# Graph passes of a GNN kernel: one TensorE event per gathered group, one or two per count stretch, where there were up to ten

## The chip, the cores and the metric

The kernel runs on one core of one Trainium2 chip. The metric is device time of the whole program in microseconds (us), the median of repeated runs. One more execution was recorded by the hardware profiler; the rows below are from it.

## The reference, cut to what matters

The program is a chain of four blocks on 6250 nodes with 256 features. The change touches only the first, a hypergraph convolution applied twice over 106250 edges (`src` to `dst`, sorted by `dst`; both directions of 50000 random pairs, and a loop at each node):

```python
def _hypergraph_conv(x, hei, W, b, num_nodes, num_edges):
    src, he = hei[0], hei[1]
    xw = x @ W.T
    deg_n = segment_sum(ones, src); deg_e = segment_sum(ones, he)
    edge_feat = b_inv[:, None] * segment_sum(xw[src], he)
    out = d_inv[:, None] * segment_sum(edge_feat[he], src)
    return out + b
...
out = _prelu(_hypergraph_conv(x, W1, b1), a)
out = _prelu(_hypergraph_conv(out, W2, b2) + x, a)
```

Each convolution is two sums over neighbours, so there are four passes over the graph, s1 to s4. A recurrent network, an attention over the same edges and a mixture of experts follow.

## The kernel before, in words

`stage_row_pass` is one pass. It makes 49 blocks of 128 summed rows in two ways, as **items**:

- A **D item** ("count stretch", 24 of them, the first 24 blocks of 128 nodes) multiplies a dense matrix of edge counts with the whole table of rows: 49 matmuls of 128x512, in 7 chunks of 7 matmuls. A chunk of counts is loaded as bf16 by SyncE (SP) into `staged` (7 slots, `CR`), widened to fp32 by ScalarE (ACT, `widen`, L621) into `ring` (3 slots, `WR`), and used by TensorE (PE, L1072).
- A **G item** ("gathered group", 54 of them) fetches 8 tiles of 128 rows by 8 indirect DMAs that GpSimd (POOL) issues (L519) into `rows` (3 buffers), and sums them by 8 one-hot matmuls (L1056). Before them one matmul "opens" the sum with the last tile of the group before (`open_sum`, L1043).

After each item, ACT copies the sum out of PSUM (L662), VectorE (DVE) scales it, and in s1, s2 and s4 PE turns the row block (L1003); in s1 and s2 it also multiplies it by a weight (`make`, L1020), ACT copies both results (L568, L575), and stores the block by a DMA (L592). These steps of earlier items stand in the middle of a later item on PE.

The order is written out by hand (`order_of_items`). In s2, s3 and s4 three G items lead, and then 2 or 3 G items stand ahead of each D item. In s1 the counts are only being built: 24 G items lead, POOL then scatters the counts by 416 indirect DMAs (L528) in four quarters, and D items 0 to 16 run as one chain, released by quarters 1 (D 0 to 4), 2 (D 5 to 10) and 3 (D 11 to 16). Then 7 D items and 30 G items are mixed, D 17 first. POOL scatters before it gathers group 24. In s1, DVE also adds the 7 chunks of a D item (`sum_chunks`, L874, L878) for the degrees.

PE tells others of its progress by semaphore increments, here called **events**. Before the change it sends, in each pass: `freed` and `group_done` for a G item (108), `a_used` for each of the 7 chunks of a D item (168), `turned` (78 in s1, s2 and s4), `made` (78 in s1 and s2), and `column_out` (24 in s1).  `freed` is what POOL waits for before it gathers into a buffer again; `a_used` is what `widen`, the loads of SP, and the copy of a D item wait for.

## Time and profile before

| | us |
|---|---|
| median of 3 runs | 6864.92 |
| lowest and highest | 6851.33, 6879.35 |
| span of the profiled execution, first to last instruction | 6729.2 |
| median less that span | 135.7 |
| PE busy, POOL busy in the span | 4418.9 (66%), 3355.7 (50%) |
| mean granted TensorE clock, share of full speed | 0.812 |

The profile gives the span alone; what lies around it is taken as the 135.7 us by which the median is above it. The four passes stand from about 60 to 3990 us. The rest of the program, to 6729 us, is not touched.

### The profile page before, as it was taken

The numbers are of one execution on the slowest core, as the hardware profiler recorded it, in microseconds if no ns is written. First come the engines' busy times: TensorE is split into PE (matmuls) and PEld (weight loads), VectorE is DVE, ScalarE is ACT, GpSimd is POOL, SyncE is SP. The second block draws the span as 40 slices with busy tenths as digits, with TensorE's granted clock in tenths as the row PEclk, the third lists the DMA queues.
The fourth block names the chain that finished last, engine by engine and source line by source line (L and its number), as shares of the span: only waits on it lengthen the run. The fifth ranks groups of instructions, "written<-read, shape, count | busy, mean of one in ns | idle before, by whom it ended". The sixth has DMA issues, their size and how long they took to land. (4 is left out here: it accounts for less than half of the span.)

```text
span 6729.2 us, 72351 instructions
## 1 busy us (share of the span) xinstructions
PE 4418.9 (66%) x20150; PEld 3518.5 (52%) x20150; DVE 2669.2 (40%) x6797; ACT 1559.4 (23%) x3386; POOL 3355.7 (50%) x3423
## 2 busy tenths in 40 slices
PE   3611139766778867876766659998546666666399
PEld 2410027554666646665555549996424444444287
DVE  7610026322222221112444342225566666666544
ACT  1100025212232222322222224333300000001233
POOL 5677730555455555655544421112466666662555
PEclk8755569878888888987888879998767777777599
DMA  7800024435444445555555550710554444444255
GB/s 265 255 18 11 11 62 120 123 107 167 128 134 131 133 148 158 162 149 167 166 166 161 154 159 0 201 38 4 147 139 117 119 118 121 118 120 118 100 88 88
DMA packets 523908, 822.38 MB, mean 122 GB/s; under 512 B 92040, under 2 KB 428367, under 8 KB 520055
## 3 DMA queue, kind: packets, MB, share of 16 engines
q0 software_dynamic: 158784, 367.62, 21.0%
q1 hardware_dynamic: 269235, 331.42, 16.5%
q10 hardware_dynamic: 95588, 120.03, 5.5%
q8 instruction: 102, 1.67, 0.1%
q14 instruction: 199, 1.63, 0.1%
HBM read 658.73 MB, written 198.82 MB: 127 GB/s over the span
## 5 line engine op out<-in xcount | busy, mean ns | idle before, releaser
L1072 PE MATMUL s_part<-both_halves,s_ring 128*128 128x512 f32 x4704 | 1330.9, 441 | 934.8 <-issue 467.3
L519 POOL DMA_INDIRECT acc<-table,ids x1296 | 1265.4, 976 | 1050.5 <-PE s_part L1043 634.7
L1072 PEld LDWEIGHTS s_part<-both_halves,s_ring 128*128 128x128 f32 x4704 | 984.3, 214 | 1217.9 <-issue 559.7
L1953 POOL DMA_INDIRECT at_rows<-h_t,ids x832 | 807.8, 971 | 470.4 <-issue 249.1
L1056 PE MATMUL s_part<-acc 128*128 128x257 f32 x3456 | 907.8, 411 | 148.5 <-DMA acc<-table,ids 59.0
L1056 PEld LDWEIGHTS s_part<-acc 128*128 128x128 f32 x3456 | 707.7, 210 | 278.2 <-DMA acc<-table,ids 64.8
L621 ACT ACTIVATE s_ring<-acc 128x896 fp32r<-128x896 bf16 x672 | 612.1, 945 | 886.3 <-remote 329.6
L519 POOL DMA_INDIRECT acc<-xn_d,ids x432 | 431.6, 999 | 495.3 <-PE s_part L1043 338.6
L2358 PE MATMUL at_part<-at_rows,at_onehot 128*128 128x264 f32 x1664 | 604.6, 493 | 4.1 <-DVE at_onehot L2175 4.1
L725 DVE TENSOR_TENSOR acc<-acc 128x256 f32<-128x256 f32 x96 | 40.9, 426 | 1376.9 <-ACT acc L662 1376.3
L528 POOL DMA_INDIRECT counted<-acc,s_place x416 | 427.2, 1027 | 132.0 <-issue 128.6
L662 ACT ACTIVATE acc<-s_part 128x257 f32<-128x257 f32 (+1 forms) x312 | 140.3, 450 | 1177.4 <-issue 316.8
L2358 PEld LDWEIGHTS at_part<-at_rows,at_onehot 128*128 128x128 f32 x1664 | 371.5, 244 | 75.1 <-issue 11.8
L1551 POOL COPY acc<-h 128x125 f32 x160 | 66.7, 417 | 598.3 <-DVE h L1579 598.3
L793 DVE TENSOR_TENSOR acc<-s_fixed,rel 128x1024 f32<-128x1024 f32 x216 | 263.9, 1222 | 195.0 <-ACT acc L662 148.5
L874 DVE TENSOR_TENSOR acc<-acc 128x896 f32<-128x896 bf16 (+1 forms) x144 | 158.2, 1098 | 430.3 <-DMA acc<-counted 361.7
L2168 DVE TENSOR_TENSOR at_rows<-at_rows,at_ps_w 128x1024 f32<-128x1024 f32 x208 | 250.7, 1205 | 34.0 <-issue 33.5
L2784 POOL DMA_INDIRECT out<-ex_y,ex_ids x112 | 178.6, 1595 | 165.1 <-DMA out<-ex_y,ex_ids 102.3
L1020 PE MATMUL s_psY<-acc 128*128 128x256 f32 x624 | 182.5, 419 | 118.2 <-issue 43.2
L1020 PEld LDWEIGHTS s_psY<-acc 128*128 128x128 f32 x624 | 123.6, 206 | 146.9 <-issue 63.7
L1995 ACT ACTIVATE at_raw<-at_part 128x264 f32<-128x264 f32 x104 | 40.6, 390 | 670.4 <-remote 246.5
L1496 PE MATMUL sw_ps<-xs,wih 128*128 x1600 | 188.3, 276 | 1.2 <-PEq L1452 1.2
(418 smaller groups left out, 6172.7 us busy)
## 6 DMA issues: line engine op xcount, KB each, us to landing
acc<-counted SPq DMA_DIRECT2D x672, 224.0 KB
xs_d<-blank SPq DMA_DIRECT2D x38, 1032.0 KB
counted<-in_x ACTq DMA_DIRECT2D x24, 1568.0 KB
table<-acc ACTq DMA_DIRECT2D x214, 128.0 KB
acc<-table,ids POOLq DMA_INDIRECT x1299
both_halves<-table SPq DMA_DIRECT2D x21, 896.0 KB, 11.9
ex_x<-xs_d SPq DMA_DIRECT2D x60, 258.0 KB
at_rows<-h_t,ids POOLq DMA_INDIRECT x832
```

The source lines that it names most:

```text
L519: pool.indirect_dma_start(rows[:, j % R, k, 0:D], None, table[0:NP_, :], bass.IndirectOffsetOnAxis(cst["ids"][:, t:t + 1], 0)).then_inc(ro ...
L528: pool.indirect_dma_start(cst["counted_flat"], bass.IndirectOffsetOnAxis(place[:, q, k:k + 1], 0), times_out[:, q, k:k + 1], None, bounds_ ...
L621: act.activation(chunk(n).bitcast(F32R), staged[:, n % CR, :], ACT.Copy).then_inc(widened, 1)
L793: dve.tensor_tensor(onehot[:, j % OG], iota.unsqueeze(1).to_broadcast([P, JT, P]), cst["rel"][:, 1, JT * g:JT * g + JT].unsqueeze(2).to_br ...
L1020: ins = pe.matmul(psY[:, 0:D], turned_x[k % 2][:, h, :], w[:, h, :], start=(h == 0), stop=(h == 1))
L1056: ins = pe.matmul(part[i % 4][:, 0:D + 1], onehot[:, k % OG, t, :], rows[:, k % R, t, 0:D + 1], start=False, stop=(t == JT - 1))
L1072: ins = pe.matmul(part[i % 4][:], chunk(n)[:, b * P:(b + 1) * P].bitcast(F32R), both[:, c * BG + b].bitcast(F32R), start=(c == 0 and b == ...
L1496: pe.matmul(ps[u][half][:, q * C:(q + 1) * C], wih[:, kk, col:col + P], xs[:, kk, bass.ds(step, 1), :].rearrange("p a c -> p (a c)"), star ...
L1953: pool.indirect_dma_start(rows[:, t % AHEAD, :], None, table, bass.IndirectOffsetOnAxis(cst["ids"][:, t:t + 1], 0)).then_inc(rows_in[t % A ...
L2168: dve.tensor_tensor(rv[:, :, 0:D].rearrange("p t (h d) -> p t h d", h=H8), rv[:, :, 0:D].rearrange("p t (h d) -> p t h d", h=H8), ps_w[:, ...
L2358: ins = pe.matmul(part[k][:, 0:W], onehot[:, t, :], row, start=(t % JT == 0), stop=False)
L2784: pool.indirect_dma_start(out, bass.IndirectOffsetOnAxis(ids[u][:, c:c + 1], 0), y[u][:, c, :], None, compute_op=ALU.add).then_inc(added[u ...
```

## The change

- PE's events: one at the end of each G item (on the next group's opening matmul, where that follows), one at the end of each D item, and for D items "in parts" one more behind their second chunk. `freed`, `a_used`, `group_done`, `turned`, `made` and `column_out` are gone; all who waited for them wait for `item_done`. Items behind the last have one event each.
- The ring has 5 slots. In s1 the first 16 D items (`LONG`) are "whole": they have 7 slots, and send one event. The two more slots lie in the gather buffers, so that group 24 isn't gathered before D item 15 is done.
- ACT widens 5 chunks of the next D item (7 where whole) at the end of the current D item, and the last two behind the event in its middle. `staged` has 5 slots (was 7), freed by `widened`, which ACT itself sends.
- A row block is turned 3 items behind its sum (was 2 in s1, s2), and multiplied and stored 5 behind (was 3).
- In s1 the degrees are turned by DVE (a copy and a 32x32 transpose), not by a PE matmul and an ACT copy; DVE finishes item i two items later; their store has 4 pieces.

```diff
-CR = 7
-WR = 3
+CR = 5
+WR = 5
+LONG = 16
...
-        LAG = 3 if kind == "last" else 2
+    R, OG, LA, LAG = 3, 3, 2, 3
+    MK = LAG + 2
...
+        def whole(win):
+            return builds and win < LONG
...
+        done = [0]
+        for i in range(NI + trailing):
+            done.append(done[i] + (2 if i < NI and in_parts(i) else 1))
+        def wait_for_part(eng, i):
+            eng.wait_ge(item_done, done[i + 1] - 1)
+        def wait_for_item(eng, i):
+            eng.wait_ge(item_done, done[i + 1])
...
                 if n >= CR:
-                    sp.wait_ge(a_used, n - CR + 1)
+                    sp.wait_ge(widened, n - CR + 1)
...
             def gather(j):
-                if j >= R - 1:
-                    pool.wait_ge(freed, j - R + 2)
+                if j >= R:
+                    wait_for_item(pool, at_g[j - R] if opens_next(j - R) else at_g[j - R + 1])
+                if builds and j == FIRST_G:
+                    wait_for_item(pool, at_d[LONG - 1])
...
             def copy_turned(k):
-                act.wait_ge(turned, k + 1)
-                if makes and k >= 2:
-                    act.wait_ge(made, k - 1)
...
             def copy_made(k):
-                act.wait_ge(made, k + 1)
...
             def widen(n):
                 act.wait_ge(a_in[n % CR], 16 * (n // CR + 1))
-                if n >= WR:
-                    act.wait_ge(a_used, n - WR + 1)
...
+                if is_d and in_parts(i):
+                    wait_for_part(act, i)
+                    for n in range(NG * win + WR, NG * win + NG):
+                        widen(n)
+                if i < NI + trailing:
+                    wait_for_item(act, i)
...
+                store_due(i)
+                if is_d and win + 1 < DW:
+                    for n in range(NG if whole(win + 1) else WR):
+                        widen(NG * win + NG + n)
...
+                        if counts:
+                            link(dve.tensor_copy(deg_col[:, 0:1], times_in))
+                            if i >= ND:
+                                wait_for_row_of(dve, i - ND)
+                            link(dve.transpose(deg_row[i % ND], deg_col))
...
-                        ins.then_inc(group_done, 1)
-                        if k + 1 < GS and at_g[k + 1] - i <= 3:
-                            open_sum(k + 1, at_g[k + 1])
+                        if opens_next(k):
+                            ins = open_sum(k + 1, at_g[k + 1])
+                        ins.then_inc(item_done, 1)
...
-                            ins.then_inc(a_used, 1)
+                            if c == NG - WR - 1 and in_parts(i):
+                                ins.then_inc(item_done, 1)
+                        ins.then_inc(item_done, 1)
```

On ACT, in the chain of D items of s1, the rows from one copy of a D sum to what follows it were these (`s_part` is the sum, `s_psT` and `s_psY` a block turned and multiplied, `s_ring` the widened counts; each row with the semaphores it waits for):

```order
L662 ACTIVATE acc<-s_part 128x512 [waits s1_scaled,s1_a_used]
L621 ACTIVATE s_ring<-acc 128x896 [waits s1_a_used,s1_a_in0]
L621 ACTIVATE s_ring<-acc 128x896 [waits s1_a_used,s1_a_in1]
L621 ACTIVATE s_ring<-acc 128x896 [waits s1_a_used,s1_a_in2]
L621 ACTIVATE s_ring<-acc 128x896 [waits s1_a_used,s1_a_in3]
L621 ACTIVATE s_ring<-acc 128x896 [waits s1_a_used,s1_a_in4]
L564 ACTIVATE acc<-s_psT 1x128 [waits s1_g_stored,s1_made,s1_turned]
L568 ACTIVATE acc<-s_psT 128x256
L575 ACTIVATE acc<-s_psY 128x257 [waits s1_g_stored,s1_made]
L621 ACTIVATE s_ring<-acc 128x896 [waits s1_a_used,s1_a_in5]
L621 ACTIVATE s_ring<-acc 128x896 [waits s1_a_used,s1_a_in6]
```

At the same place of the changed kernel (L675 is the copy, L591 and L596 the other two copies, L613 and L616 the stores, L640 the widening):

```order
L675 ACTIVATE acc<-s_part 128x512 [waits s1_scaled,s1_item_done]
L591 ACTIVATE acc<-s_psT 128x256
L596 ACTIVATE acc<-s_psT 128x256 [waits s1_g_stored]
L613 ISA [waits s1_g_stored,s1_made_out]
L613 DMA table<-acc 128x256
L616 REGISTER_ALU [waits s1_ready]
L616 DMA deg_d<-acc 4x32
L640 ACTIVATE s_ring<-acc 128x896 [waits s1_a_in4]
L640 ACTIVATE s_ring<-acc 128x896 [waits s1_a_in0]
L640 ACTIVATE s_ring<-acc 128x896 [waits s1_a_in1]
L640 ACTIVATE s_ring<-acc 128x896 [waits s1_a_in2]
L640 ACTIVATE acc_counts<-acc 128x896 [waits s1_a_in3]
```

One wait for PE is left for a D item, where each widening had one; all widening stands behind the stores now.

On ACT in s2, around one D item, the rows before were:

```order
L662 ACTIVATE acc<-s_part 128x257
L621 ACTIVATE s_ring<-acc 128x896 x2
L568 ACTIVATE acc<-s_psT 128x256
L575 ACTIVATE acc<-s_psY 128x256
L621 ACTIVATE s_ring<-acc 128x896 x2
L592 DMA table<-acc 128x256
L662 ACTIVATE acc<-s_part 128x512
L621 ACTIVATE s_ring<-acc 128x896 x3
```

and in the changed kernel, from the copy of the G item ahead:

```order
L675 ACTIVATE acc<-s_part 128x257
L591 ACTIVATE acc<-s_psT 128x256
L596 ACTIVATE acc<-s_psT 128x256
L613 DMA table<-acc 128x256
L640 ACTIVATE acc_counts<-acc 128x896
L640 ACTIVATE s_ring<-acc 128x896
L675 ACTIVATE acc<-s_part 128x512
```

Two chunks, not four, are widened while the D item runs.

## Rows read from the trace of the kernel before

**Rows 1.** Busy us of PE, PEld, DVE, ACT, POOL in s1 to s4; clock, DMA.
```profile
60.00:1560.00 1500.00, 732.73 (x2820) 543.48 (x2820) 475.01 (x765) 256.79 (x487) 856.40 (x846) 0.73 0.34 100
1560.00:2402.00 842.00, 643.86 (x2621) 520.16 (x2621) 214.57 (x494) 244.79 (x410) 422.24 (x433) 0.87 0.47 138
2402.00:3122.00 720.00, 550.70 (x2148) 438.97 (x2148) 134.84 (x329) 195.71 (x253) 421.29 (x434) 0.88 0.53 156
3122.00:3990.00 868.00, 583.98 (x2298) 464.36 (x2299) 375.40 (x1017) 227.60 (x403) 424.68 (x432) 0.82 0.56 164
```
**Rows 2.** Waits of POOL for PE in s2, s3, s4: total us, times, longest.
```profile
POOL acc L519 <- PE s_part L1043: 238.5, 22, 15.8
...
POOL acc L519 <- PE s_part L1043: 121.3, 18, 15.6
...
POOL acc L519 <- PE s_part L1043: 274.8, 22, 17.2
```
**Rows 3.** Timeline of POOL: scatter begins, gathering of group 24 begins, two restarts.
```profile
343.42 1.03 POOL L528 DMA_INDIRECT counted<-acc,s_place  x1 [3.33 <-DVEq L849]
...
899.53 0.99 POOL L519 DMA_INDIRECT acc<-xn_d,ids  x1 [0.30 <-issue]
...
1168.92 0.95 POOL L519 DMA_INDIRECT acc<-xn_d,ids  x1 [248.53 <-PE s_part L1043]
...
1523.04 0.94 POOL L519 DMA_INDIRECT acc<-xn_d,ids  x1 [13.86 <-PE s_part L1043]
```
**Rows 4.** Timeline of ACT in the scatter: start, duration, idle time before and releaser.
```profile
538.30 0.27 ACT L564 ACTIVATE acc<-s_psT 1x128 f32<-1x128 f32 x1 [40.29 <-issue]
...
616.70 0.60 ACT L662 ACTIVATE acc<-s_part 128x512 f32<-128x512 f32 x1 [57.79 <-issue]
...
781.96 0.60 ACT L662 ACTIVATE acc<-s_part 128x512 f32<-128x512 f32 x1 [57.85 <-remote]
```
**Rows 5.** Timeline of SP's load issues in the scatter, and busy time there.
```profile
557.90 0.32 SPq L498 DMA_DIRECT2D acc<-counted  x1
...
597.10 0.32 SPq L498 DMA_DIRECT2D acc<-counted  x1
...
343.00:895.00 552.00, 72.27 (x201) 49.71 (x199) 34.97 (x47) 24.74 (x41) 423.85 (x413) 0.55 0.06 12
```
**Rows 6.** Timeline of s1 with POOL silent (923 to 1160).
```profile
1051.46 5.01 PE L1072 MATMUL s_part<-both_halves,s_ring 128*128 128x512 f32 x21 [1.62 <-ACT s_ring L621]
...
1064.66 0.60 ACT L662 ACTIVATE acc<-s_part 128x512 f32<-128x512 f32 x1 [3.75 <-PE s_part L1072]
...
1079.46 0.60 ACT L662 ACTIVATE acc<-s_part 128x512 f32<-128x512 f32 x1 [3.76 <-PE s_part L1072]
```
**Rows 7.** Timeline of one D item of s3 while POOL issues three groups.
```profile
2661.29 5.14 PE L1072 MATMUL s_part<-both_halves,s_ring 128*128 128x512 f32 x21
...
2669.73 0.95 ACT L621 ACTIVATE s_ring<-acc 128x896 fp32r<-128x896 bf16 x1 [6.70 <-DMA acc<-in_x]
2680.25 0.95 ACT L621 ACTIVATE s_ring<-acc 128x896 fp32r<-128x896 bf16 x1 [9.56 <-DMA acc<-in_x]
```
**Rows 8.** Two openings of G items in s2, back to back.
```profile
1856.04 0.60 PE L1043 MATMUL s_part<-acc 128*128 128x257 f32 x2
...
1861.03 0.60 PE L1043 MATMUL s_part<-acc 128*128 128x257 f32 x2
```
**Rows 9.** L1072 in 1640:2380 (s2), 2500:3100 (s3), 3190:3940 (s4).
```profile
L1072 PE MATMUL s_part<-both_halves,s_ring x1114: 387/393/796, 1639.4 to 2368.4; 128*128 128x512 f32 x186
...
L1072 PE MATMUL s_part<-both_halves,s_ring x1078: 387/389/797, 2508.5 to 3090.5; 128*128 128x512 f32 x180
...
L1072 PE MATMUL s_part<-both_halves,s_ring x1079: 387/392/988, 3196.6 to 3939.7; 128*128 128x512 f32 x180
```
**Rows 10.** Timeline of POOL: one gather instruction in s3, and the idle time before it.
```profile
2740.61 0.95 POOL L519 DMA_INDIRECT acc<-table,ids  x1 [0.30 <-issue]
```
**Rows 11.** Waits of PE in s4, 3190:3940, before turning a block.
```profile
PE s_psT L1003 <- issue: 63.0, 12, 11.7
```

More of the change, by code:

```diff
@@ L343, in stage_row_pass @@
     counts = degrees is not None and kind == "edge"
+    trailing, late = MK if makes else LAG if turns else 0, 2 if builds else 0
     per_store = 32 if counts else 16
@@ L378, in stage_row_pass @@
             psY = m.ps(f"{name}_psY", [P, 512])
-            y = [room.take(D + 1) for _ in range(NY)]
-        if counts:
-            deg_row = [room.take(P)[0:1, :] for _ in range(2)]
+            y = [room.take(D) for _ in range(NY)]
         if kind != "edge":
@@ L997, in turn @@
                     pe.wait_ge(turned_out, k - 1)
[L998 to L1001 removed]
+                frm = x[k % NX] if makes else row[b]
                 for h in range(2):
                     ins = pe.transpose(psT[b][:, h * P:(h + 1) * P], frm[:, h * P:(h + 1) * P], cst["ident"][:])
[L1004 removed]
@@ L1006, in column_of, with make @@
-            def column_of(k, narrow):
-                if not narrow:
-                    pe.matmul(psY[:, D:D + 1], cst["ident"][:], cst["ones"][:, 0:1], start=True, stop=True)
-                    return
+                return ins
+            def make(k):
+                pe.wait_ge(turned_out, k + 1)
+                if k >= 2:
+                    pe.wait_ge(made_out, k - 1)
+                for h in range(2):
+                    ins = pe.matmul(psT[k % 2][:, D:2 * D], turned_x[k % 2][:, h, :], w[:, h, :], start=(h == 0),
+                                    stop=(h == 1))
+                return ins
@@ L1010, in column_of, with make_and_turn @@
+            def make_and_turn(i):
+                if makes and MK <= i < NI + MK:
+                    ins = make(i - MK)
+                if turns and LAG <= i < NI + LAG:
+                    ins = turn(i - LAG)
+                if i >= NI:
+                    ins.then_inc(item_done, 1)
+            def column_of(i):
+                k = items[i][1]
                 pe.wait_ge(column_ready, k + 1)
-                pe.matmul(psY[:, D:D + 1], total_sum, cst["ones"][:, 0:1], start=True, stop=True).then_inc(column_out, 1)
@@ L1013, in make @@
-            def make(k, narrow):
-                pe.wait_ge(turned_out, k + 1)
                 if k:
-                    pe.wait_ge(made_out, k)
-                if with_column(k):
-                    column_of(items[k + 2][1], narrow)
-                for h in range(2):
-                    ins = pe.matmul(psY[:, 0:D], turned_x[k % 2][:, h, :], w[:, h, :], start=(h == 0), stop=(h == 1))
-                ins.then_inc(made, 1)
-            def make_and_turn(i, narrow=True):
-                if makes and i >= 3:
-                    make(i - 3, narrow)
-                if turns and LAG <= i < NI + LAG:
-                    turn(i - LAG, narrow)
+                    pe.wait_ge(scaled, at_d[k - 1] + 1)
```

229 lines of the change are left out of this document (110 added, 119 removed).

## Prediction

> **What bounds the kernel now.** I first read the busy time by pass [rows 1]. The passes take 1500, 842, 720 and 868 us, and nothing in them is busy throughout: in s2, PE works 644 of 842 us and POOL 422. (POOL's 0.30 us between two DMAs belongs to its pace: one gather instruction takes 0.95 + 0.30 = 1.25 us [rows 10], a group of 8 takes 10.0, and 54 groups 540.) The reader is to see that s2, s3 and s4 stand 180 to 330 us above POOL's 540.
>
> The table of waits came second [rows 2]: POOL waits for PE 238 us in s2, 121 in s3, 275 in s4. So PE is late, though it is idle for a quarter of the time. Why it is late shows in the timeline [rows 7]. A D item starts at 2661.29 and does 3 chunks in 5.1 us. The fourth and fifth chunk need a ring slot, freed by `a_used` of the first and second, which PE had finished by about 2664.7. ACT, idle, goes on at 2669.73 and at 2680.25: 7 to 16 us after the matmuls that it waits for. The counts had long been loaded. What is late is PE's event.
>
> The scatter of s1 shows the same with a rhythm [rows 4, 5]. SP issues its loads every 19.6 us (557.90 to 597.10 in two steps), each when one more `a_used` reaches it, and ACT copies a D sum at 616.70 and at 781.96, 165.3 us apart. PE is busy 72 of 552 us there [rows 5]. A D item sends 10 events in this stretch (7 `a_used`, `turned`, `made`, `column_out`), and 165.3 us is 8.4 times 19.6. With POOL silent, the copy at 1064.66 follows the last matmul by less than 0.1 us, and a D item takes 14.8 us [rows 6]. So I read it thus: while POOL issues DMAs, PE's events go out one by one, at 19.6 us in the scatter and some 5 to 10 us in a long run of gathers [rows 7], and PE's own number of events sets the pace.
>
> **A rule that speaks against this.** The Trainium skill (TensorE: Matmul & The Clock Gate, "The cost: per-tile semaphore tail") says that increments by matmuls serialize at 26.3 ns each. The change takes away about 1118 events, and by that rule this would be worth 29 us, an estimate from that page. By the trace one event costs up to 19.6 us [rows 5]. The trace and the page differ by far more than a hundred times while POOL is busy. With POOL silent the trace [rows 6] does not contradict the page.
>
> **Count of events.** Before: 54 x 2 + 24 x 7 = 276 in s3; with `turned` 354 in s4, with `made` too 432 in s2, with `column_out` 456 in s1: 1518. After: 54 + 2 x 24 = 102 in s3 and s4, 107 in s2, and in s1 54 + 16 + 2 x 8 + 5 = 91: about 400.
>
> **Prices of PE's work at full clock.** 21 count matmuls take 5.01 us [rows 6], so 49 take 11.7. A G item of s2 takes 1861.03 - 1856.04 = 4.99 us [rows 8], with one make and turn. PE's busy time differs between s2 and s3 by (643.9 - 550.7)/78 = 1.2 us an item and between s4 and s3 by 0.4 [rows 1]. So s2: G 5.0, D 12.9; s3: G 3.8, D 11.7; s4: G 4.2, D 12.1.
>
> **s1, until group 24 is gathered.** The scatter stands from 343 to 899.5 [rows 3] and is unchanged. D 0 starts at 478. A whole D item sends one event. After it ACT copies the sum (0.60), two blocks, issues two stores and widens the first chunk (0.95): about 3.5 us before PE can go on, since whole items share all 7 slots; before, the next item's first chunks stood ready but for the ring. With PE's 12.9 and a little this is 17 us an item with POOL silent, against 14.8 now: a loss. In the scatter I add 2.5 us for matmuls at a lower clock, and for the event half of 19.6: 29.3 us, against 165. D 0 to 4 end at 625, D 5 to 10 (released well before) at 801, and by 899.5 14.4 of the 16 items are done, where now fewer than 3 are. The rest takes 1.6 x 17 = 27: group 24 is gathered from 927. Bounds: event at once, 899.5 (all 16 are done at about 881); event after the full 19.6, 39 us an item, 10.8 done, 5.2 x 17 more: 988.
>
> **s1, the 30 groups behind.** Now POOL restarts at 1168.92 with 28 to go and restarts last at 1523.04 [rows 3]: (1533 - 1169)/28 = 13.0 us a group. Every two groups it waits. With fewer events I expect three groups between waits of 3 us, that is (3 x 10.3 + 3)/3 = 11.3, taken as 11.2; a group is 10.3 us here, 8 x (0.99 + 0.30) [rows 3]. 927 + 30 x 11.2 = 1263 against 1533: **-270**. Bounds: 899.5 + 30 x 10.3 = 1209 (-324), and 988 + 30 x 13 = 1378 (-155).
>
> **s2, s3, s4.** One D item comes with 2.25 G items. The time of such a stretch now is the window over (count of matmuls / 49) [rows 9]: s2 740/22.7 = 32.6 us, s3 600/22.0 = 27.3, s4 750/22.0 = 34.1. After:
> - s2: PE 2.25 x 5.0 + 12.9 = 24.1. The event in the middle of D is sent 3.4 us in, comes after up to 8 us [rows 7], and ACT widens in 1: 12.4, while five chunks cover 8.4 + 1.2. So 3 us of stall remain: 27.1. Over 24 stretches **-132**. Bounds: no stall, 24.4 (-195); stall 6 (-60).
> - s3: PE 2.25 x 3.8 + 11.7 + 3 = 23.3, but POOL needs 22.6, plus a wait of 2.5 us for every two groups: 25.4, **-46**. Bounds: POOL without waits 23.1 (-100); no gain.
> - s4: 2.25 x 4.2 + 12.1 = 21.6, plus 3 and the 63 + some us that PE waits before turning [rows 11], 4.4 a stretch with what stands beside it. That rests on DVE's chain of ten steps, not on events alone, so I keep it and half a microsecond more for ACT: 29.5, **-110**. Bounds: POOL's 25.4 (-208), and -60.
>
> **Small terms.** Two more widenings before the first item of three passes, 2 x 0.95 x 3 = 6; two more trailing items in s1 and s2, some 1.5 us each: **+12** in all. The degrees on DVE cost two short instructions an item, hidden: DVE is busy 475 of 1500 us [rows 1]. Staging 5 slots, not 7, costs nothing while loads land 2 us after their issue and are freed by ACT's own events; if cover were gone, two loads (4 us) for each D item, 24 x 4 a pass.
>
> **Sum.** -270 - 132 - 46 - 110 + 12 = -546. The profiled span of 6729.2 becomes 6183, and with the 135.7 us around it the median 6319.
>
> **Rivals.**
> - *POOL alone bounds.* Events no longer queue at all: all four upper bounds, -827 + 12, so about 6050; with half of that extra gain 6185. For it: short stretches of the trace where events come within 1 us. Against it: a POOL that never waits is just where events were slowest.
> - *The scatter does not speed up.* If it is the loads that take 19.6 us there (224 KB each; only 12 GB/s are moved), D items keep their pace and s1 gains only 28 x 1.8 = 50. Total -326, 6539. Against it: once issued, loads land in about 2 us, and ACT's copy, which needs no load, keeps the same rhythm [rows 4].
> - *Events cost only themselves* (the page's rule). Nothing but tens of ns for each of 1118: 6835, no measurable change. The trace speaks against it [rows 4, 7].
> - *Slower: POOL's longer runs starve the one event that a D item needs.* Today a D item gets through because POOL stops every two groups. If the event in its middle comes only when POOL stops, after three groups, a stretch takes 3 x 10 + 3, and the next D the same: some 36 us in s2 and s4, 36 in s3: 24 x (3.4 + 8.7 + 1.9) = +336; less s1's 270 that is +66, 6930. It decides from 546/80 = 6.8 us of extra stall for each of the 80 D items in parts, so from about 9.8 us each.
>
> **Chances.** The forecast (6200 to 6450) 0.58; POOL alone bounds 0.18; scatter unchanged 0.15; events cost only themselves 0.05; slower 0.04. The range 6100 to 6580 leaves out the last two and the far end of the second. A measurement of this kernel can't tell less than about 0.5% (34 us) from no change: faster 0.91, same 0.05, slower 0.04.
>
> **What the profile after would show.** Right: copies of D sums (L675, 512 wide) every 25 to 40 us in the scatter, not 165; group 24 gathered by 900 to 990, s1 ended by about 1300; POOL's waits in s2 and s4 halved; PE's stalls before the sixth chunk some 3 us. Wrong: D items still 100 us or more apart in the scatter; POOL in runs of three groups with PE idle more than 8 us within each D item; or PE waiting on `psT` and `made_out` in s2 as it waits now for the ring.

## The result and the profile after

The changed kernel takes 6753.68 us (median of 4, 6734.97 to 6758.35), where the kernel before took 6867.65 us in the same comparison: a ratio of 0.9837, interval 0.9812 to 0.9861. It is 114 us (1.7%) faster, where 546 us were forecast.

The same kernel takes a different time on different chips: the kernel before was met at about 6868, at 6720 to 6745, and at 5495 to 5500 us. So every ratio below is to the kernel before on the same chip. "The 5500 us chips" names the last kind (B in some expectations, where A is the 6868 us kind); it needs a reading of its own.

The page of the changed kernel, its first line:

```profile
span 6733.3 us, 71038 instructions
```

The time of that execution is 6734.97 us, so only 1.7 us lie around a span. The 135.7 us that the prediction took for "around the span" were not that: the profiled execution of before was itself some 134 us shorter than those timed.

Windows by pass of the changed kernel, answering [rows 1], with the same columns (busy us of PE, PEld, DVE, ACT, POOL, then clock, DMA share, GB/s):

```profile
60.00:1604.00 1544.00, 725.67 (x2664) 557.24 (x2664) 498.91 (x899) 235.31 (x409) 839.13 (x846) 0.71 0.33 97
1604.00:2410.00 806.00, 655.24 (x2621) 514.87 (x2621) 213.02 (x494) 235.73 (x410) 419.99 (x433) 0.88 0.47 144
2410.00:3136.00 726.00, 572.49 (x2148) 446.92 (x2148) 134.79 (x329) 189.43 (x253) 420.20 (x433) 0.85 0.50 155
3136.00:3960.00 824.00, 576.60 (x2258) 459.25 (x2259) 374.33 (x1012) 217.57 (x400) 427.10 (x433) 0.83 0.57 173
```

Against [rows 1], pass s1 is longer by about 44 us, s2 and s4 are shorter by about 36 and 44, and s3 is 6 longer. That does not add up to 114 us, and the two spans are nearly the same (6729.2 and 6733.3): the profile of before is of a shorter execution than its timed runs, so this comparison can't place the gain. Waits of POOL for PE, in s2, s3 and s4 of the changed kernel, answering [rows 2]:

```profile
POOL acc L549 <- PE s_part L1065: 205.4, 22, 12.9
...
POOL acc L549 <- PE s_part L1065: 128.0, 18, 15.6
...
POOL acc L549 <- PE s_part L1065: 235.1, 23, 14.4
```

They are as many as before (22, 18 and 22 then), and their sum is 14% smaller in s2 and s4. The halving that was forecast for s2 and s4 is not to be seen. Nor are three groups between waits in s1: in the 28 groups from 1206 us on, POOL waits 14 more times.

ACT's copies of D sums in the scatter of the changed kernel, answering [rows 4]:

```profile
608.40 0.60 ACT L675 ACTIVATE acc<-s_part 128x512 f32<-128x512 f32 x1 [121.91 <-remote]
768.34 0.60 ACT L675 ACTIVATE acc<-s_part 128x512 f32<-128x512 f32 x1 [151.47 <-remote]
924.13 0.60 ACT L675 ACTIVATE acc<-s_part 128x512 f32<-128x512 f32 x1 [147.35 <-remote]
```

and the busy time there, answering [rows 5]:

```profile
343.00:895.00 552.00, 67.96 (x191) 45.15 (x191) 30.86 (x44) 22.59 (x33) 400.52 (x408) 0.53 0.06 12
```

This is the finding of the profile after. A D item in the scatter now sends one event, and not ten, and the copies still stand 159.9 us apart, where they stood 165.3 apart (the third came at 924.13, when the scatter had ended). The timeline of PE between the first two copies shows why:

```profile
611.97 7.10 PE L1100 MATMUL s_part<-both_halves,s_ring 128*128 128x512 f32 x21 [91.22 <-issue]
618.91 1.02 PE L1031 MATMUL s_psT<-acc 128*128 128x256 f32 x4
619.77 0.38 PE L1023 MATMUL s_psT<-ident,s_x 128*128 128x128 f32 x2
619.91 1.85 PE L1100 MATMUL s_part<-both_halves,s_ring 128*128 128x512 f32 x7
...
632.53 0.59 PE L1100 MATMUL s_part<-both_halves,acc_counts 128*128 128x512 f32 x1 [2.21 <-issue]
635.33 0.58 PE L1100 MATMUL s_part<-both_halves,acc_counts 128*128 128x512 f32 x1 [2.21 <-issue]
...
680.13 0.58 PE L1100 MATMUL s_part<-both_halves,acc_counts 128*128 128x512 f32 x1 [2.22 <-issue]
```

PE has all operands: all 7 chunks of a whole item are widened before its last matmuls. It takes some 35 instructions at its own speed, and then one every 2.80 us, with nothing that it waits for by the profile ("issue"). The last one starts at 680.13, and its event reaches ACT at 768.34: 87.6 us after the end, or 31 times 2.80 (one item earlier the same: from 520.16 to 608.40). I read this so: ends are told every 2.80 us, and PE starts instructions some 31 ahead of those whose end is told. The count of instructions here is that of the trace: a count matmul is one, while a matmul by a one-hot matrix, by the weight or for the degrees stands as two (L1056 has 3456, which is 2 x 8 for each of 216 groups). So a D item has 49 matmuls and, from L1031, L1023 and the sum for the degrees (L1049), 4 + 2 + 2 more: 57 x 2.80 = 159.6, measured 159.9. Before it had 59: 165.2, measured 165.3.

POOL in the changed kernel, answering [rows 3]: the scatter's last instruction, the start of groups 24 and 25, the restart with group 26, and the first gather of s2:

```profile
904.51 0.98 POOL L558 DMA_INDIRECT counted<-acc,s_place  x1 [0.41 <-issue]
1159.25 0.99 POOL L549 DMA_INDIRECT acc<-xn_d,ids  x1 [253.77 <-PE s_part L1100]
...
1206.13 0.95 POOL L549 DMA_INDIRECT acc<-xn_d,ids  x1 [27.03 <-PE s_part L1065]
...
1604.30 0.95 POOL L562 DMA_INDIRECT acc<-table,ids  x1 [29.91 <-POOLq L356]
```

Two of the sixteen whole D items are done at the end of the scatter, a third soon after it, and group 26 starts 37 us later than it did (1168.92 in [rows 3]).

With POOL silent, each of the other thirteen takes 18.0 us on average (copies from 924.13 to 1158.47), where an item took 15.0 (943.68 to 1138.65). PE at the start of one of them, and the windows 960:1150 of before and of the changed kernel:

```profile
1018.78 6.66 PE L1100 MATMUL s_part<-both_halves,s_ring 128*128 128x512 f32 x21 [3.28 <-ACT s_ring L640]
...
960.00:1150.00 190.00, 168.98 (x758) 131.74 (x757) 121.45 (x155) 98.99 (x143) 0.00 (x0) 1.00 0.43 117
...
960.00:1150.00 190.00, 153.30 (x595) 122.08 (x594) 106.83 (x143) 78.81 (x110) 0.00 (x0) 0.87 0.33 100
```

PE is idle for 3.28 us there, where it was for 1.62 [rows 6], because the first widening of the next item stands behind ACT's two copies and two stores. The next 21 matmuls then take 6.66 us and not 5.01, and the granted clock of that stretch is 0.87, where it was 1.00.

### The profile page after: what moved, and what is told of

It reads as the page before. It is cut to its first block and busy times, and to the rows that moved or that the text cites. A ratio compares the mean times of both kernels' runs of the same rounds, so it can differ in the third digit from the quotient of the medians.

```text
span 6733.3 us, 71038 instructions
## 1 busy us (share of the span) xinstructions
PE 4446.3 (66%) x19994; PEld 3536.5 (53%) x19994; DVE 2693.7 (40%) x6935; ACT 1515.0 (23%) x3308; POOL 3342.7 (50%) x3423
## 5 line engine op out<-in xcount | busy, mean ns | idle before, releaser
L1100 PE MATMUL s_part<-both_halves,s_ring 128*128 128x512 f32 x3598 | 1029.0, 435 | 748.5 <-issue 494.1
L1100 PEld LDWEIGHTS s_part<-both_halves,s_ring 128*128 128x128 f32 x3598 | 743.9, 210 | 978.7 <-issue 705.1
L1082 PE MATMUL s_part<-acc 128*128 128x257 f32 x3456 | 988.7, 432 | 322.7 <-issue 162.2
L1082 PEld LDWEIGHTS s_part<-acc 128*128 128x128 f32 x3456 | 734.7, 219 | 501.5 <-issue 216.5
L675 ACT ACTIVATE acc<-s_part 128x257 f32<-128x257 f32 (+1 forms) x312 | 138.5, 447 | 2095.0 <-remote 1004.4
L640 ACT ACTIVATE s_ring<-acc 128x896 fp32r<-128x896 bf16 x514 | 455.2, 938 | 545.4 <-remote 180.7
L558 POOL DMA_INDIRECT counted<-acc,s_place x416 | 409.8, 985 | 155.0 <-issue 155.0
L1100 PE MATMUL s_part<-both_halves,acc_counts 128*128 128x512 f32 x1106 | 326.8, 429 | 171.0 <-issue 138.0
L1100 PEld LDWEIGHTS s_part<-both_halves,acc_counts 128*128 128x128 f32 x1106 | 223.3, 205 | 235.2 <-issue 157.5
L1065 PE MATMUL s_part<-acc 128*128 128x257 f32 x432 | 142.3, 411 | 70.2 <-issue 23.7
```

Source lines behind the costliest of these rows:

```text
L558: pool.indirect_dma_start(cst["counted_flat"], bass.IndirectOffsetOnAxis(place[:, q, k:k + 1], 0), times_out[:, q, k:k + 1], None, bounds_ ...
L640: act.activation(chunk(n).bitcast(F32R), staged[:, n % CR, :], ACT.Copy).then_inc(widened, 1)
L1082: ins = pe.matmul(part[i % 4][:, 0:D + 1], onehot[:, k % OG, t, :], rows[:, k % R, t, 0:D + 1], start=False, stop=(t == JT - 1))
L1100: ins = pe.matmul(part[i % 4][:], chunk(n)[:, b * P:(b + 1) * P].bitcast(F32R), both[:, c * BG + b].bitcast(F32R), start=(c == 0 and b == ...
```

## The experiments

### One question: what is paced, events or instructions?

**More events.** The kernel before, with one more increment on each of 6 of a chunk's 7 matmuls, 42 for a D item, 4032 in all:

```diff
+        extra = m.sem(f"{name}_extra")
...
+                                if b < BG - 1:
+                                    ins.then_inc(extra, 1)
```

The expectations call the prediction's reading E (events are paced) and the new one M (ends of instructions are paced). The first is that of the unchanged kernel, run to learn where the 134 us between its profile and its timed runs lie. It met a 5500 us chip, so it could not answer that; more_events met such chips three times.

> The kernel before, unchanged, to see where its time stands in an execution near its median. The profile of before that the prediction used spans 6729 us, 138 us below the median of 6868, and the changed kernel's spans 6733. Both theories (E: while GpSimd issues DMAs, TensorE's events go out one by one and their number sets the pace; M: what is slow is the completion of each TensorE instruction, 2.8 us in the scatter, whatever it signals) expect about 6850 to 6880 us here, with the 110 to 140 us more somewhere between 60 and 3990 us; if the span is again near 6730, the gain of the change is not in the passes at all.

> The kernel before, with 42 more semaphore increments in each D item (on every count matmul that had none, on a semaphore for which nobody waits). E: in the scatter a D item sends 52 events, not 10, and takes 52 x 19.6 = 1020 us or at least several times 165; the program is slower by hundreds of us or more. M: the number of instructions is the same, D items stay 165 us apart in the scatter, and the time stays within 1% of before.

> The kernel before with 42 more increments in each D item (4032 in all). On B they cost 2 us in all at most, as before (5497 against 5495). On A: E expects D items in the scatter several times the 165 us apart, and hundreds of us more; M expects 165 us and a time within 1% of before.

> The kernel before with 42 more increments in each D item. On B again within 8 us of before. On A: E expects D items in the scatter several times the 165 us apart, and hundreds of us more; M expects 165 us and a time within 1% of before.

Measured: unchanged 5495.64; with more events 5497.22, 5502.83 and 5508.66 us, where the kernel before took 5495.29, 5496.63 and 5500.24. That is 2 to 8 us for 4032 events, at most 2.1 ns each, from single runs and hardly outside the spread of the kernel before (5489 to 5505), and on these chips nothing of PE is late in the scatter in the first place: D copies stand 14.8 us apart there too. So this could not tell the theories apart. A chip of the other sort was met later.

> The kernel before with 42 more increments of a semaphore per wide item, 4032 in all. If this chip is one where the kernel before takes about 6870 us: by events being paced, the copies of wide items in the scatter stand several hundred us apart; by each instruction's end being paced, they stand 165 us apart as before and the time is within 20 us of the kernel before. If it is one where the kernel before takes about 5500 us: no difference of over 10 us by either.

Measured: 6755.67 us, the kernel before 6743.41; ratio 1.0019 (0.9990 to 1.0048). Timeline of PE in the scatter, from one D item's first matmul to the last one before the next copy (L1073 counts, L1012 and L1001 the sums of degrees and their turn, L1021 multiply, L1004 turn):

```profile
616.60 6.35 PE L1073 MATMUL s_part<-both_halves,s_ring 128*128 128x512 f32 x21 [55.96 <-ACT s_ring L622]
635.68 0.59 PE L1012 MATMUL s_psY<-ones,acc 128*128 128x1 f32 x2 [12.73 <-ACT s_ring L622]
636.13 2.06 PE L1021 MATMUL s_psY<-acc 128*128 128x256 f32 x4
638.12 0.58 PE L1001 MATMUL s_psT<-ident,acc 128*1 128x128 f32 x2
638.63 0.69 PE L1004 MATMUL s_psT<-ident,acc 128*128 128x128 f32 x2
638.97 2.28 PE L1073 MATMUL s_part<-both_halves,s_ring 128*128 128x512 f32 x7
655.28 3.35 PE L1073 MATMUL s_part<-both_halves,s_ring 128*128 128x512 f32 x7 [14.03 <-issue]
703.51 3.35 PE L1073 MATMUL s_part<-both_halves,s_ring 128*128 128x512 f32 x7 [44.87 <-issue]
722.48 3.36 PE L1073 MATMUL s_part<-both_halves,s_ring 128*128 128x512 f32 x7 [15.62 <-ACT s_ring L622]
```

and of ACT, the two copies around it:

```profile
615.02 0.60 ACT L663 ACTIVATE acc<-s_part 128x512 f32<-128x512 f32 x1 [57.79 <-issue]
780.28 0.60 ACT L663 ACTIVATE acc<-s_part 128x512 f32<-128x512 f32 x1 [57.85 <-remote]
```

52 events instead of 10, and the copies are 165.26 us apart as before, to the hundredth. Events are not what is paced. The rows of PE sum to 59 instructions, and 59 x 2.80 = 165.2. The 19.6 us on which I built fit the same: a chunk has 7 matmuls, 7 x 2.80 = 19.6.

**Fewer instructions.** The changed kernel with 4 of the 7 matmuls of each chunk. It leaves out 3 of 7 blocks of nodes.

```diff
-                            for b in range(BG):
+                            for b in range(BG - 3):
```

> The changed kernel with 4 of the 7 matmuls of each count chunk (28 a D item, 21 left out of 49, so the counts of 3 blocks of nodes in 7 are left out of the sums). Events and loads are as in the changed kernel. M: in the scatter a D item is 28 + 8 = 36 TensorE instructions of 2.8 us, so 101 us from copy to copy, not 160. E or loads: 155 to 160 us stays. In s2 to s4 both expect less time, 21 x 0.24 = 5 us a D item by TensorE's work alone (-360 us over 72 items), M more than that where GpSimd is issuing.

> The changed kernel with 4 of the 7 matmuls of each count chunk (21 of 49 left out, so 3 blocks of nodes in 7 are left out of the sums). On A: M expects 36 instructions x 2.8 = 101 us from copy to copy in the scatter, E 155 to 160. On B: 5481 again.

On 5500 us chips it took 5481.49 and 5490.27 us, 14 and 6 below the kernel before and 85 and 76 below the changed kernel (5566.25 on one such chip, below), where the expectation had 360 less in s2 to s4: PE's own work is not all that bounds the passes there. On a 6868 us chip:

> The changed kernel with 4 of the 7 matmuls of each chunk (it leaves out 3 of 7 blocks of nodes), so a wide item has 36 of TensorE's instructions and not 57. If the end of each instruction is paced at 2.80 us in the scatter: copies of wide items 101 us apart there. If something per item or per event is paced: 160 us apart as before. On a chip without the pacing: as in the runs before, within 15 us of the kernel before.

Measured: 6393.05 us, ratio 0.9312 (0.9276 to 0.9348). Timeline of ACT in its scatter:

```profile
654.74 0.60 ACT L675 ACTIVATE acc<-s_part 128x512 f32<-128x512 f32 x1 [92.67 <-remote]
755.84 0.60 ACT L675 ACTIVATE acc<-s_part 128x512 f32<-128x512 f32 x1 [92.67 <-remote]
```

101.1 us apart (the next is 101.2 later), and 36 x 2.80 = 100.8. Nothing per item, per chunk, per load or per event fits 165.3, 159.9 and 101.1; 2.80 us for each instruction fits all three.

It reaches further than the scatter. Beside the changed kernel on the same chip (6763.02 us) the run is 370 us shorter: s1 ends 116 us sooner, and s2, s3 and s4 are 110, 78 and 63 us shorter. On the 5500 us chips the same edit makes them 34, 8 and 25 us shorter (four_of_seven2 beside after_again). So the number of PE's instructions also costs more in the gather passes where ends are told late.

**A quarter of the scatter.** The changed kernel with 104 scattering DMAs for 416. It leaves out three quarters of the counts.

```diff
-                        sp.wait_ge(scattered[q], 16 * QT)
+                        sp.wait_ge(scattered[q], 16 * (QT // 4))
...
-                for k in range(QT):
+                for k in range(QT // 4):
```

> The changed kernel with a quarter of the scatter's instructions, 104 for 416 (it leaves out three quarters of the counts). Theory (TensorE's instructions end late while GpSimd scatters, and by that alone): the scatter takes about 140 us and not 565; at most one wide item's copy comes late, the others stand 17.6 us apart from then on, and the run is 350 to 450 us faster than the changed kernel. Rival (something else of that stretch paces them, the loads of counts or the stretch of the program): the copies stand 160 us apart behind the scatter's end too, and the gain is under 200 us.

Measured: 6364.21 us, beside 6763.02 for the changed kernel on the same chip: 399 us less. POOL's last scattering DMA, and the first two D copies:

```profile
470.25 0.98 POOL L558 DMA_INDIRECT counted<-acc,s_place  x1 [0.30 <-issue]
...
505.27 0.60 ACT L675 ACTIVATE acc<-s_part 128x512 f32<-128x512 f32 x1 [9.79 <-PE s_part L1100]
523.19 0.60 ACT L675 ACTIVATE acc<-s_part 128x512 f32<-128x512 f32 x1 [9.45 <-PE s_part L1100]
```

17.9 us apart as soon as the scatter is over, and 17.4 to 19.1 for the ones that follow (once 23.7). The pacing goes with the scatter. It shows that POOL's scatter, with what it sets off, slows the ends of PE's instructions on such a chip; it does not show by which path. POOL's own pace is not what differs between chips: it issues the 416 DMAs of the scatter 1.34 us apart on average in the kernel before here, and 1.32 us apart on a 5495 us chip (base_again2).

### Where the gain lies, and what holds the gather passes

> The changed kernel, unchanged. On a chip where TensorE's instructions end late in the scatter (the kernel before near 6745 us): 1.5 to 1.9% faster than the kernel before, 6620 to 6645 us, and no more than 10 us from the kernel with a third turned buffer. If that kernel's 1.5% came from its two edits instead, the changed kernel takes 6720 us or more there. On the other kind of chip 5560 to 5570 us again.

Measured: 6763.02 us, the kernel before 6867.82; ratio 0.9850 (0.9811 to 0.9890). The result stands. The chip was one of the 6868 us kind, not 6745, so the times of the expectation don't apply, the ratio does.

> The kernel before, unchanged, for a profile beside its timed runs. On a chip where it takes 6740 us or more: the pass with the scatter ends 20 to 40 us earlier than in the changed kernel (wide items 14.8 us apart behind the scatter, not 17.6), and the second and the fourth pass are longer by 30 to 50 and by 60 to 80 us. If the gain lies elsewhere, behind the four passes, these differences do not sum to it.

Measured: 6727.97 us; the profiled execution took 6747.49, with a span of 6745.8. Its pass lengths are near those of [rows 1]. Against the changed kernel's two profiles, s1 ends 21 to 23 us sooner, as expected, but s2 is only 4 to 25 us longer and s4 33 to 39, less than expected; those profiles are from 6868 us chips.

The passes, read off POOL's timeline, in us (from the second gathering DMA of a pass to that of the next; s1 from the start of the span; s4 to the end of its last gather):

| kernel, time of before on its chip | s1 | s2 | s3 | s4 |
|---|---|---|---|---|
| before, the profile of the rows | 1564.8 | 843.5 | 713.9 | 833.8 |
| before (unchanged_slow_chip), 6720 | 1583.0 | 836.2 | 715.3 | 833.2 |
| changed, the profile after, 6868 | 1605.5 | 811.2 | 724.9 | 793.9 |
| changed (changed_again), 6868 | 1603.9 | 832.7 | 728.4 | 799.9 |
| early_widening, 6720 | 1597.0 | 807.7 | 710.7 | 752.3 |
| third_turned_again, 6720 | 1597.4 | 804.7 | 704.7 | 756.8 |
| whole_three_turned, 6868 | 1603.8 | 817.9 | 730.8 | 773.2 |
| before (base_again2), 5495 | 1207.6 | 618.6 | 578.3 | 578.8 |
| changed (after_again), 5497 | 1207.8 | 622.4 | 579.9 | 630.7 |
| widen_first, 5500 | 1205.3 | 623.9 | 580.3 | 613.1 |

On a chip of the 6720 to 6745 us kind there is a second pair of profiles: beside more_events5, which is the kernel before but for its increments, third_turned (below) ends s1 18 us later and has s2, s3 and s4 shorter by 46, 15 and 70 us.

One cycle of POOL in s2 of the changed kernel shows what is late in a gather pass. The timeline, from the first three chunks of a D item; POOL had started two groups at 1978.33:

```profile
1982.69 5.14 PE L1100 MATMUL s_part<-both_halves,s_ring 128*128 128x512 f32 x21
...
1987.02 1.79 ACT L640 ACTIVATE s_ring<-acc 128x896 fp32r<-128x896 bf16 x2 [3.00 <-PE s_part L1100]
...
1993.82 1.52 PE L1100 MATMUL s_part<-both_halves,s_ring 128*128 128x512 f32 x6
...
1995.52 0.69 PE L1082 MATMUL s_part<-acc 128*128 128x257 f32 x2 [0.18 <-issue]
...
1996.94 0.38 PE L1082 MATMUL s_part<-acc 128*128 128x257 f32 x1 [0.72 <-issue]
...
1998.34 0.77 PE L1082 MATMUL s_part<-acc 128*128 128x257 f32 x2 [1.03 <-issue]
...
2001.39 0.60 ACT L675 ACTIVATE acc<-s_part 128x512 f32<-128x512 f32 x1 [12.59 <-remote]
...
2007.48 0.95 POOL L549 DMA_INDIRECT acc<-table,ids  x1 [9.15 <-PE s_part L1065]
```

The event in the middle of the D item comes at once here, and the item runs through to 1995.3 without a stall. Then the last event takes until 2001.4, and the G item behind it starts its matmuls singly, 1.4 us apart, until some 3 us after POOL's run of two groups has ended. POOL then waits 9.15 us for that G item. I read it as the same thing as in the scatter, shorter: PE is held behind ends that are told late. That is one cycle; four_of_seven4 is what supports it for the passes as a whole.

What did change in these passes are PE's waits. In s2, PE waits for widened chunks 13 us in all in 1650:2370 of the changed kernel, where it waited 70 in 1640:2380; its waits at the same matmuls for which the profile shows no cause ("issue") rose from 57 to 80. In s4, one line of 3190:3940 of before, and two of 3180:3940 of the changed kernel:

```profile
PE s_part L1072 <- ACT s_ring L621: 82.2, 20, 9.6
...
PE s_part L1100 <- ACT s_ring L640: 85.5, 10, 12.6
...
PE s_psT L1023 <- issue: 20.4, 11, 3.3
```

The waits for widened chunks are not shorter in s4 (with `acc_counts` 102.5), but those ahead of turning a block fell from 100 us (63.0 of them in [rows 11]) to 25. The second profile of either kernel (unchanged_slow_chip, changed_again) has the same: 84 to 13 us for chunks in s2, 108 to 34 ahead of turning in s4. No run takes the parts of the change one by one, so which of them shortened these waits is not shown.

**Early widening.** On the 5500 us chips the changed kernel is slower, and s4 is where (630.7 for 578.8):

> The changed kernel, unchanged. The last runs showed two kinds of chip: one (call it A) on which before takes 6868 us and TensorE's instructions complete late while GpSimd issues DMAs, and one (B) on which before takes 5495 us and nothing is late. On A I expect the measured 0.984 again, on B 1.013 to 1.02: nothing is won where nothing is late, and s4 and the whole D items of s1 are longer (with three whole items it was 1.0128). Theory E (the number of events is what costs) and M (every instruction's completion costs) can't be told apart by this run; that the gain is the kernel's own and holds everywhere would need a ratio below 1 on both.

Measured: 5566.25 us, ratio 1.0126 (1.0109 to 1.0143). Waits in 2460:2980 (s4) of it:

```profile
ACT acc L591 <- DMA xt_d<-acc: 109.4, 21, 7.4
...
PE s_part L1100 <- ACT s_ring L640: 37.1, 14, 5.2
```

and the timeline of one D item of it:

```profile
2738.17 0.60 ACTq L632 DMA_DIRECT2D xt_d<-acc  x1
2738.88 1.79 ACT L640 ACTIVATE s_ring<-acc 128x896 fp32r<-128x896 bf16 x2 [7.04 <-issue]
...
2739.88 6.28 PE L1100 MATMUL s_part<-both_halves,s_ring 128*128 128x512 f32 x14 [4.10 <-ACT s_ring L640]
```

ACT stands at the stores of the G item ahead (a store waits for the landing of the one before), and the last two widenings of the D item stand behind them, so PE waits 4.1 us. The edit puts them first:

```diff
+                if not is_d and i + 1 < NI and in_parts(i + 1):
+                    widen_last(i + 1)
                 store_due(i)
```

> The changed kernel with one thing moved on ScalarE: the wait for the event in the middle of a D item and the two widenings behind it come ahead of the stores of the G item before, not behind them. Theory S (stores): in s4 on chip B the change loses 55 us because these two widenings wait behind two stores that wait for earlier stores to land; it expects s4 back at some 575 to 585 us from 632, the sixth chunk's stall (4 us a D item) gone, and a ratio near 1.000 to 1.004 on B, where the changed kernel has 1.0126; on A 15 to 40 us less than the changed kernel. Rival R (ring): the event comes too late for two chunks whatever stands before them; the stall stays above 3 us and the ratio at 1.01.

Measured: 5549.65 us, ratio 1.0091 (1.0074 to 1.0108): about 17 to 20 us of the 70 come back, 17.6 of them in s4, which now takes 613 us and not the 575 to 585 expected. PE's waits for `s_ring` in 2460:2980 fell from 37.1 to 18.5 us, so only half of them went. The stores ahead of the widening are a part of the loss on these chips, and the smaller one. On a 6720 us chip:

> The changed kernel with the two late widenings of a wide item ahead of the stores of the item before it. If these edits are worth on this chip what they gave on the other (16 us of 5566), it takes 10 to 25 us less than the changed kernel, a ratio to the kernel before of 0.981 to 0.983. If TensorE's ends hide them there: 0.985, as the changed kernel.

Measured: 6636.70 us, where the kernel before took 6719.80; ratio 0.9880 (0.9827 to 0.9934). Against the profile of the kernel before on that chip, s1 is 14.0 longer, s2, s3 and s4 are 28.5, 4.6 and 80.9 shorter, and what is behind them 7 shorter: together the 107 us by which the spans differ (6745.8 and 6638.6). So for this version the loss in s1 and the gains in s2 and s4 are both seen. In s4, PE's waits for `s_ring` are 29.8 us in 3170:3850, where the changed kernel has 85.5 and 114.8 in its two profiles. Yet the ratio is neither in the expected 0.981 to 0.983 nor below what the changed kernel has on 6868 us chips; on this kind of chip the changed kernel itself wasn't measured.

**A third turned buffer**, beside the early widening, so that ACT's copy of a turned block waits for the landing three items back:

```diff
-                if kind == "last" and k >= 2:
-                    wait_for_turned_of(act, k - 2)
-                put = turned_x[b] if makes else xt[b]
+                if kind == "last" and k >= 3:
+                    wait_for_turned_of(act, k - 3)
+                put = turned_x[b] if makes else xt[k % 3]
```

> The kernel with the two late widenings ahead of the stores, and in the fourth pass three buffers for turned blocks in place of two, so that ScalarE waits for the landing of the block three items back. Theory (what is left of the fourth pass' loss is ScalarE held at the turned blocks' landing, 137.0 us in that kernel's stretch against 73.5 in the kernel before): that wait falls under 60 us, and the pass ends 20 to 30 us sooner, 5520 to 5530 us where the kernel before takes 5500. Rival (the landing only takes the place of another wait, and GpSimd's gathers, one group further on, set the end): the wait falls and the time stays, 5545 to 5555 us. On a chip where TensorE's instructions end late in the scatter no difference of over 10 us to the changed kernel is expected from this, and the kernel before takes over 6800.

> The same with three buffers for turned blocks. If the 43 us of the kernel with 3 whole windows came from the widening and the third buffer: a ratio to the kernel before of 0.978 to 0.980. If they came from the number of whole windows: 0.983 to 0.986.

Measured: 6643.19 us, ratio 0.9849 (0.9809 to 0.9890), and 6641.57, ratio 0.9878 (0.9833 to 0.9923), on the chip where early widening alone has 6636.70. The third buffer gives nothing there, and 0.9878 is above both ranges of the expectation, nearer to the one in which the number of whole items brings the gain. It met no 5500 us chip, so whether it would give back more of s4 there is open.

**Three whole items for sixteen**, so that POOL gathers groups 24 and 25 behind the third D item: `LONG = 3` for `LONG = 16`.

> The changed kernel with LONG = 3: only the three D items that end before the scatter does are whole, the 13 behind have 5 chunks widened ahead and two events. In the changed kernel a whole item takes 17.6 us with GpSimd silent where one of before took 14.8. Both theories: 12 items x 2.8 = 34 us less in s1 than the changed kernel, ratio to before about 0.979; in the scatter nothing changes. If it is not faster than the changed kernel, ScalarE's widening behind the event isn't what makes whole items long.

Measured on a 5500 us chip, on the changed kernel: 5563.98 us, ratio 1.0128 (1.0111 to 1.0145), no gain where 34 us were expected. Its D items in parts are as slow as the whole ones:

```profile
664.98 5.04 PE L1100 MATMUL s_part<-both_halves,s_ring 128*128 128x512 f32 x14 [3.27 <-ACT s_ring L640]
```

PE waits the same 3.3 us at their start, and copies stand 17.4 to 19.1 us apart within a quarter. So it is not the single event that makes an item long; with one event or two, the next item's first chunk is widened only behind the last event, the copies and the stores. With early widening and the third buffer, on a 6868 us chip:

> The kernel with early widenings and three turned buffers, and besides 3 whole windows in place of 16 in the first pass, so that GpSimd starts its next gathers behind the third wide item and not behind the sixteenth. Theory (the 254 us that GpSimd waits at its restart put off the end of the first pass): it is 30 us or more faster than the kernel with 16. Rival (the first pass ends with TensorE's work, and the wide items and their parts cost the same wherever they stand): within 10 us of it.

Measured: 6719.85 us, ratio 0.9779 (0.9747 to 0.9810), 43 us under the changed kernel on the same chip. But s1 ends at the same time to 0.1 us. POOL gathers its two groups 230 us sooner, from 930.63, and then waits for the same thing:

```profile
1211.26 0.94 POOL L550 DMA_INDIRECT acc<-xn_d,ids  x1 [260.81 <-PE s_part L1071]
```

Its wait of 254 us had cost only those two groups' place; PE's chain of D items ends when it ends. The edit of `LONG` touches s1 alone, so by the profiles the gain lies elsewhere: s4 is 21 to 27 us shorter than in the two profiles of the changed kernel, which fits the early widening. In s2 (817.9) it lies between those two (811.2 and 832.7), so nothing is shown there. This is the fastest version measured on such a chip; on the 5500 us chips none of them beats the kernel before.

## Why the prediction was wrong, point by point

- **The step that failed** is the reading "PE's events go out one by one, and PE's own number of events sets the pace". What is paced is the end of each PE instruction: 2.80 us each in the scatter. I had divided 165.3 by 19.6 and taken the 8.4 for roughly ten events. It is 59/7 = 8.43 to the second digit: 59 instructions an item, 7 a chunk. That events are many and late together was no evidence for their number. The single steps of 2.80 us are not to be seen in PE's timeline of before, since its three slots let it start only seven matmuls at a time; the exact ratio was.
- **s1, -270.** D items in the scatter were priced at 29.3 us and take 159.9. Two were done at its end, as before, and not 14.4. With the scatter's part gone, the loss that the prediction named was left, and its mechanism was right: 3.3 us before PE can go on (3.5 forecast), and 18.0 us an item (17 forecast). What it left out is that the clock falls from 1.00 to 0.87 with it. Group 26 starts 37 us later, by this sum from the copies: the third D item 20 sooner, the next thirteen 39 longer, D 16 and 17, the first of them beside POOL's new gathers, 12 longer, and from there to POOL's restart 5 more, since the event stands now at the end of the group. The 28 groups behind take (1574.4 - 1206.1)/28 = 13.2 us each, not 11.2, against 13.4 before (the prediction had 13.0, since it took one group behind the restart at 1523.04, where two follow, to 1542.8). At its end the pass waits 9 us longer. Together s1 ends 39 to 41 us later than in the profile of the rows, and 14 later with early widening on its own chip.
- **s2, -132, and s4, -110.** Measured 11 to 32 and 34 to 40 less, comparing the two profiles of the changed kernel with the first row of the table. The stall in the middle of a D item, priced at 3 us, was not there in the cycle of s2 shown, and 13 us in the whole pass; PE was held at the item's end and behind it instead. In s4 it was larger than priced (102.5 us over 22 items, 4.7 each), while the wait ahead of turning, which the prediction kept, shrank. POOL waited as often as before.
- **s3, -46.** Measured 11 to 15 more by that comparison; early widening and the third buffer have 5 to 11 less on their chip.
- **The page's rule** (the Trainium skill, TensorE: Matmul & The Clock Gate, "The cost: per-tile semaphore tail": 26.3 ns an increment, serialized; the page gives it for the tail behind a burst of tiled matmuls). I set it aside because the trace seemed to show up to 19.6 us an event, and those were the ends of 7 instructions. By that rule of the Trainium skill 4032 more increments would be worth 106 us, an estimate from that page. Measured were 2 to 12 us (the last with an interval from 7 less to 32 more), beside other work: no run here shows 26.3 ns for each, and nothing of 19.6 us an event is left.
- **The rivals.** Nearest by time was "events cost only themselves" (6835, 0.05), 81 us above the result. Its statement on events came true, but it gives no gain, and 114 us were measured; beyond the waits shown above no run says where those come from. "The scatter does not speed up" (6539, 0.15) had the outcome of the scatter right, with another cause than the loads; its time was 215 us too low, since it kept the gains of s2 to s4 at the price of the failed step. "POOL alone bounds" was further off. The slower case (6930) did not come on this chip; on the 5500 us chips the change is slower, but not by the mechanism priced. The range of 6100 to 6580 rested on one reading, and all its bounds varied sizes within it. That the kernel got faster at all was forecast, but for a reason that did not hold: it was luck in that sense.
- **What stays open.** By what path POOL's DMAs hold up PE's ends, and why only on some chips. Whether the unit is a matmul or a matmul with its weight load: each has one (191 and 191 in the window above), so no run tells them apart. Whether the recording has a part in it: every timed run has a recorded span, so there is none without it. Which parts of the change bring the gain. How the 105 to 114 us split over the passes on a 6868 us chip: no profile of the kernel before was taken there, since the profiled execution of the rows lies 134 us under the timed ones and matches a 6720 to 6745 us chip, which is an inference from its pass lengths. Why whole_three_turned has a ratio of 0.978 on a 6868 us chip, and the same without `LONG = 3` 0.985 and 0.988 on the 6745 and 6720 us ones, with s1 unchanged. And what holds s4 at 613 us on the 5500 us chips after early widening, where the kernel before has 579; ACT's wait for the landing of turned blocks was larger (137.0 for 73.5 us in 2460:2980), but its removal was not run there.

## What to carry to other kernels

When an engine's signals come late, count what the delay is a multiple of, instructions, events, chunks or loads, exactly, and in two places, before pricing a change by one of them: here 165.3 is to 19.6 as 59 instructions to 7, and 10 events to 1 do not fit. Where ends of PE's instructions are late, fewer instructions helped (36 for 57 took a D item from 160 to 101 us), and fewer signals did not (1 for 10: from 165 to 160, and those by two instructions less). Waits made coarser to save signals cost their own 3 us an item as soon as nothing is late. And a version tuned on one chip should be timed on more than one: the same change was 1.6% faster on one and 1.3% slower on another.

## What the runs showed of the hardware that I had not expected

- While POOL scatters by indirect DMAs, on some chips the ends of PE's instructions come 2.80 us apart, a multiplying one or a turn alike, and PE starts some 31 instructions ahead of them (the last event 87.6 us behind the last matmul). On others, under the same program, a D item in the scatter takes 14.8 us.
- The kernel before takes 6868, 6720 to 6745 or 5495 to 5500 us by the chip. In s2 POOL's wait for PE is then 238.5 us (in 1640:2380, [rows 2]) or 24.4 (in 1230:1780, on a 5495 us chip), and the clock over the pass 0.87 or 0.96.
- 4032 more semaphore increments on matmuls cost 2 to 12 us, within the noise or hardly outside it.
- With POOL silent, PE's idle stretch of 3.3 us instead of 1.6 in each D item went with a granted clock of 0.87 instead of 1.00 (960:1150), and 21 matmuls behind it took 6.66 us instead of 5.01.
